# First experts in pairs of turns, with the weighted parts added by GpSimd

## The reference, cut to what matters

```python
def _L0_ffn_ref(x, gate_w, gate_b, w1, b1, w2, b2, gamma, beta):
    B, S, H, F, E, K = (8, 1024, 64, 128, 16, 2)
    gate_logits = x @ gate_w + gate_b
    topk_vals, topk_idx = jax.lax.top_k(gate_logits, K)
    topk_w = jax.nn.softmax(topk_vals, axis=-1)
    h = jax.nn.relu(jnp.einsum('bsh,ehf->bsef', x, w1) + b1)
    expert_out = jnp.einsum('bsef,efh->bseh', h, w2) + b2
    sel = jnp.take_along_axis(expert_out, topk_idx[:, :, :, None], axis=2)
    moe = jnp.sum(topk_w[..., None] * sel, axis=2)
    y = x + moe
    return layernorm(y) * gamma + beta
```

## Time and profile before

| what | value |
|---|---|
| runs shown, us | 741.77, 748.18, 747.81; median 747.81 |
| span of the profiled execution, us | 745.7 |
| TensorE busy, us (share) | 652.7 (88%) |
| VectorE busy | 570.2 (76%) |
| ScalarE busy | 502.8 (67%) |
| GpSimd busy | 334.1 (45%) |
| first experts: weightings L1132, 64 | 48.0 us busy, 750 ns each |
| first experts: VectorE's adds L1091, 56 | 44.1 us busy, 788 ns each on average |
| transfers mid<-spread_w, 128 | 128 KB each, 2.8 us from issue to landing |

### The profile page before, as it was taken

How to read it: one execution, slowest core, us unless ns; L and a number is a source line. 1 busy time by engine, 2 the same in 40 slices (tenths; PEclk the granted TensorE clock), 3 DMA queues, 4 the chain that set the end, 5 groups by cost and what they waited for, 6 DMA issues and landing times.

```text
span 745.7 us, 16401 instructions
## 1 busy us (share of the span) xinstructions
PE 652.7 (88%) x4984; PEld 364.3 (49%) x4984; DVE 570.2 (76%) x1633; ACT 502.8 (67%) x1264; POOL 334.1 (45%) x417
## 2 busy tenths in 40 slices
PE   5528998999999988999999997699888988889896
PEld 5514654666666654323333324365555655565332
DVE  6676787777777774798999988669888888867653
ACT  3746877888888872576777767658777777744542
POOL 1006578788787875133333333725445644320000
PEclk9857999999999997999999999699999999987999
DMA  4030000000000001433333330000000000000001
GB/s 109 1 113 1 1 2 1 0 0 0 0 0 0 1 0 66 161 106 108 109 113 115 107 109 14 3 1 2 1 0 0 0 0 0 1 1 1 16 20 23
DMA packets 22038, 24.37 MB, mean 33 GB/s; under 512 B 12390, under 2 KB 12902, under 8 KB 21734
## 3 DMA queue, kind: packets, MB, share of 16 engines
q1 hardware_dynamic: 19751, 23.31, 10.3%
q10 hardware_dynamic: 2239, 0.49, 0.3%
HBM read 22.48 MB, written 1.31 MB: 32 GB/s over the span
## 4 chain that ended last, share of the span: by engine, by line
PE 59%; DVE 19%; issue 8%; ACT 4%; POOL 2%; DMA 1%; DVEq 0%; SPq 0%; ACTq 0%; POOLq 0%
PE ps L723 8%; PE ps L759 7%; PE ps L1551 5%; PE ps L641 4%; PE ps L1573 4%; PE ps L717 4%; DVE big L1091 4%; PE ps L652 3%; DVE big L2062 3%; DVE big L1132 2%; PE ps L1557 2%; PE ps L1802 2%; PE ps L709 2%; PE ps L1824 2%; PE ps L705 2%
## 5 line engine op out<-in xcount | busy, mean ns | idle before, releaser
L1338 POOL TENSOR_TENSOR big<-big 128x1024 f32<-128x1024 f32 x64 | 119.9, 1895 | 45.3 <-DVE big L1152 45.3
L939 ACT ACTIVATE big<-ps,big 128x255 f32<-128x255 f32 x256 | 117.3, 485 | 11.4 <-DVE big L1146 8.9
L901 ACT ACTIVATE big<-ps,b1s 128x512 f32<-128x512 f32 x128 | 80.3, 679 | 40.1 <-PE ps L641 38.9
L1146 DVE TENSOR_REDUCE big<-ps 128x4 f32<-128x1020 f32 x64 | 75.2, 1213 | 27.3 <-PE ps L717 27.3
L1920 ACT ACTIVATE big<-ps 128x1024 f32<-128x1024 f32 x64 | 65.9, 1030 | 32.9 <-PE ps L1563 30.5
L2062 DVE TENSOR_REDUCE big<-ps 128x4 f32<-128x1020 f32 x64 | 78.1, 1220 | 6.8 <-DVE res L2119 2.5
L723 PE MATMUL ps<-cst,big 128*128 128x128 f32 x512 | 77.5, 285 | 6.3 <-POOL big L1338 2.4
L1158 DVE COPY mid<-ps 128x512 f32<-128x512 f32 x96 | 63.5, 686 | 18.7 <-PE ps L723 15.4
L641 PE MATMUL ps<-big,wall 64*128 64x512 f32 x256 | 75.7, 656 | 0.7 <-ACT big L872 0.7
L723 PEld LDWEIGHTS ps<-cst,big 128*128 128x128 f32 x512 | 54.9, 141 | 40.8 <-issue 20.8
L652 PE MATMUL ps<-big,w2s 128*64 128x512 f32 x256 | 70.8, 632 | 1.2 <-ACT big L901 1.2
(11 more groups left out here) (274 smaller groups left out, 1342.2 us busy)
## 6 DMA issues: line engine op xcount, KB each, us to landing
mid<-spread_w SPq DMA_DIRECT2D x128, 128.0 KB, 2.8
mid<-in_split_sel SPq DMA_DIRECT2D x1, 1536.0 KB, 7.5
wall<-in_w SPq DMA_DIRECT2D x1, 1280.0 KB, 6.2
out_tokens<-res SPq DMA_DIRECT2D x16, 56.0 KB, 1.6
cst<-in_consts SPq DMA_DIRECT2D x1, 520.5 KB, 5.1
pexp<-in_w_raw SPq DMA_DIRECT2D x1, 512.0 KB, 6.2
w2s<-in_w SPq DMA_DIRECT2D x1, 512.0 KB, 3.4
mid<-in_taps ACTq DMA_DIRECT2D x1, 320.0 KB, 3.9
```

What stands on the lines that cost most here:

```text
L901: last = nc.scalar.activation(hid[e % 2][j], H1(e, j), ACT.Relu, bias=b1s[0][:, 2 * e + j:2 * e + j + 1])
L939: last = nc.scalar.activation(e_sb[r % 4][:, jj, tq, 0:NW], S[:, 2 * (r % 2) + jj, tq, 0:NW], ACT.Exp, scale=-1.0, bias=minus[r % 4][:, jj ...
L1146: nc.vector.tensor_reduce(minus[r % 4], S[:, 2 * a:2 * a + 2, :, 0:NW], AX.X, ALU.min).then_inc(s_mx, 1)
L1338: nc.gpsimd.tensor_tensor(e_sb[r % 4], e_sb[r % 4], bc(inverse[r % 4].unsqueeze(3), [P, 2, 2, 256]), ALU.mult).then_inc(s_A, 1)
```

## The change

The diff, cut to its core. First the buffers and TensorE:

```diff
-            TURN_SUM, COLUMNS, LOGITS, GAP, WEIGHTS = 1, 6, 0, 2, 6
+            PARTS, ADDS = 4, DUOS - 1
+            GAP = 3
             tile = lambda first, n=512: big[:, first:first + n]
-            hid = [[tile(1024 * e + 512 * j) for j in range(2)] for e in range(2)]
-            part, acc = ([tile(2048 + 1024 * m + 512 * n) for n in range(2)] for m in range(2))
+            hid = [[tile(first + 512 * j) for j in range(2)] for first in (0, 1024, 4352, 5376)]
+            part = [tile(first) for first in (2048, 2560, 7936, 8448)]
+            acc = [tile(3072 + 512 * n) for n in range(2)]
...
                 def sum_turn(c, q, last_chunk=False):
-                    pe.wait_ge(s_acc, c + 1)
+                    pe.wait_ge(s_added, ADDS * (c + 1))
...
                 def duos(c, q):
                     known = isinstance(c, int)
-                    for e in range(DUOS):
-                        s = DUOS * c + e
-                        if e < DUOS - 1:
-                            hidden(q, e + 1, s + 1)
-                        elif not known or c < CH - 1:
-                            pe.wait_ge(s_xc, c + 2)
-                            hidden(1 - q, 0, s + 1)
-                        if e == WEIGHTS and (not known or c < CH - 1):
+                    for g in range(DUOS // 2):
+                        s = DUOS * c + 2 * g
+                        if g == DUOS // 2 - 1 and (not known or c < CH - 1):
                             weights(c + 1)
-                        second(e, s)
-                        if e == COLUMNS and (not known or c < CH - 2):
-                            if known and c == 0:
-                                pe.wait_ge(s_O, B)
-                            columns_of(c + 2)
-                        if e == LOGITS and (not known or c < CH - 1):
+                            if not known or c < CH - 2:
+                                if known and c == 0:
+                                    pe.wait_ge(s_O, B)
+                                columns_of(c + 2)
+                        for e in (2 * g + 2, 2 * g + 3):
+                            if e < DUOS:
+                                hidden(q, e, DUOS * c + e)
+                            elif not known or c < CH - 1:
+                                pe.wait_ge(s_xc, c + 2)
+                                hidden(1 - q, e - DUOS, DUOS * c + e)
+                        if g == 0 and (not known or c < CH - 1):
                             logits(c + 1, 1 - q)
-                        if e == TURN_SUM and (not known or c >= 1):
+                        second(2 * g, s)
+                        second(2 * g + 1, s + 1)
+                        if g == 0 and (not known or c >= 1):
                             sum_turn(c - 1, 1 - q, known and c == CH - 1)
```

ScalarE's `duos`: with four `hid` buffers a ReLU waits for the second product four turns back; the gap's exponential goes behind turn 3, the own scaling to turns 6 and 7, the copies of weights and columns behind turn 7:

```diff
-                        if not known or s >= 2:
-                            act.wait_ge(s_w2, s - 1)
+                        if not known or s >= 4:
+                            act.wait_ge(s_w2, s - 3)
...
-                        if e == 5 and c >= 1:
-                            own_scale(c - 1, (0, 1))
-                        if e == WEIGHTS and (not known or c < CH - 1):
+                        if e in (6, 7) and c >= 1:
+                            own_scale(c - 1, ((0, 1), (2, 3))[e - 6])
...
+                        if e == 7 and c < CH - 1:
                             weights(c + 1, 1 - q)
-                        if e == 6 and c >= 1:
-                            own_scale(c - 1, (2, 3))
+                        if e == 7 and c < CH - 2:
+                            columns_out(c + 2, q)
```

VectorE's `duos`, which no longer adds:

```diff
-                        if e == 1 and c >= 1:
-                            dve.wait_ge(s_acc, c)
-                        nc.vector.scalar_tensor_tensor(out=acc[q] if e == 0 else part[e % 2], in0=Y(e), scalar=b2s[:, e:e + 1], in1=cb[e % RING],
+                        n = ADDS * c + e - 1
+                        if e >= 1 and n >= PARTS:
+                            dve.wait_ge(s_added, n - PARTS + 1)
+                        nc.vector.scalar_tensor_tensor(out=acc[q] if e == 0 else part[n % PARTS], in0=Y(e), scalar=b2s[:, e:e + 1], in1=cb[e % RING],
                                                        op0=ALU.add, op1=ALU.mult).then_inc(s_m, 1)
-                        if e >= 2:
-                            add_part(c, q, e - 1)
-                        elif e == 0 and c >= 1:
-                            add_part(c - 1, 1 - q, DUOS - 1)
```

GpSimd's `duos`:

```diff
+                def add_part(c, e):
+                    n = ADDS * c + e - 1
+                    pool.wait_ge(s_m, DUOS * c + e + 1)
+                    if e >= 2:
+                        pool.wait_ge(s_added, n)
+                    nc.gpsimd.tensor_tensor(acc[c % 2], acc[c % 2], part[n % PARTS], ALU.add).then_inc(s_added, 1)
+
                 def duos(c):
                     if c < CH - 2:
                         fetch_chunk(c + 2)
+                    add_part(c, 1)
+                    add_part(c, 2)
                     if c >= 1:
                         own_root(c - 1)
+                    add_part(c, 3)
...
                     for h in ((0, 1), (2,), (3,), (4,), (5,), (6,), (7,), ())[c]:
                         pos_scores(h)
+                    add_part(c, 4)
+                    add_part(c, 5)
                     if c >= 2:
                         next_root(c - 2)
+                    add_part(c, 6)
+                    add_part(c, 7)
```

More of the change, by code:

```diff
@@ L582, in attention0_and_experts0 @@
             zb = small[:, 5:5 + H]
-            s_h, s_hid, s_w2, s_m, s_acc = (sem("e0_" + n) for n in ("hidden", "activated", "second_done", "weighted", "summed"))
+            s_h, s_hid, s_w2, s_m, s_added = (sem("e0_" + n) for n in ("hidden", "activated", "second_done", "weighted", "part_added"))
             s_cd, s_cb = sem("e0_weights_in_dram"), [sem(f"e0_spread{n}") for n in range(RING)]
@@ L651, in second @@
                     for j in range(2):
-                        last = nc.tensor.matmul(Y(e)[D * j:D * j + D], w2s[0][:, 2 * e + j], hid[e % 2][j], start=True, stop=True)
+                        last = nc.tensor.matmul(Y(e)[D * j:D * j + D], w2s[0][:, 2 * e + j], hid[e % 4][j], start=True, stop=True)
                     last.then_inc(s_w2, 1)
                 def sum_turn(c, q, last_chunk=False):
-                    pe.wait_ge(s_acc, c + 1)
+                    pe.wait_ge(s_added, ADDS * (c + 1))
                     if not last_chunk:
@@ L840, in _ @@
                 weights(0)
+                hidden(0, 1, 1)
                 duos(0, 0)
@@ L897, in duos @@
                         act.wait_ge(s_h, s + 1)
-                        if not known or s >= 2:
-                            act.wait_ge(s_w2, s - 1)
+                        if not known or s >= 4:
+                            act.wait_ge(s_w2, s - 3)
                         for j in range(2):
-                            last = nc.scalar.activation(hid[e % 2][j], H1(e, j), ACT.Relu, bias=b1s[0][:, 2 * e + j:2 * e + j + 1])
+                            last = nc.scalar.activation(hid[e % 4][j], H1(e, j), ACT.Relu, bias=b1s[0][:, 2 * e + j:2 * e + j + 1])
                         last.then_inc(s_hid, 1)
[L903 to L907, removed]
                         if e in (1, 2) and c >= 3:
@@ L911, in duos @@
                             gap(c + 1)
-                        if e == 5 and c >= 1:
-                            own_scale(c - 1, (0, 1))
-                        if e == WEIGHTS and (not known or c < CH - 1):
+                        if e in (6, 7) and c >= 1:
+                            own_scale(c - 1, ((0, 1), (2, 3))[e - 6])
+                        if e in (3, 7) and c >= 1:
+                            for h in (((0,), (1,)) if c == 1 else ((c,), ()))[e // 4]:
+                                pos_exps(h)
+                        if e == 7 and c < CH - 1:
                             weights(c + 1, 1 - q)
-                        if e == 6 and c >= 1:
-                            own_scale(c - 1, (2, 3))
+                        if e == 7 and c < CH - 2:
+                            columns_out(c + 2, q)
                 def columns_first():
@@ L1086, in finish @@
                     return [total, stats, own.variance, gain, add]
[L1088 to L1095, removed]
                 def pos_max(h):
@@ L1269, in _ @@
                     duos(c, c % 2)
-                add_part(CH - 1, 1, DUOS - 1)
                 later.finish, later.next_norm = finish, next_norm
```

## The result

Four runs of each kernel on one chip gave 761.8 us after the change (757.0 to 764.2) and 744.8 before (741.4 to 748.2): a ratio of 1.0222, 95% interval 1.018 to 1.0264. The change makes the kernel slower: the whole interval lies above 1. The profiled execution of after has a span of 762.3 us against 745.7, 16.6 more.

A forecast was written before the change was run, and what follows sets the result against it. TensorE and VectorE were both taken as nearly full. 745.7 + 12.5 (six loops) + 2 (chunk 0) = 760.2 us profiled; the median lies 2.1 above the span, so 762. Forecast's own range 756 to 767, overall 747 to 776.

The forecast's parts named there:

- The two holds: VectorE's L455 and shares' step wait for GpSimd's adds 2 and 3 on SBUF: +0.81 and +1.12 us per loop.
- The stall moved from the sum's turn to the weights' turn: TensorE, counted from S, the sum's turn's start: ready at 9.29, waits for weights; loop 20.5 us without holds, 22.4 with.
- Putting products side by side I cost at nothing: First experts on TensorE: pairing first and second products saves nothing; a pair of turns keeps four products, floor 19.58 per chunk.
- a first product behind a first product well under 1.06: Sign on TensorE that, if seen in the profile, would show the forecast wrong altogether.
- Little idle before the sum's turn: Profile sign on TensorE: little idle there, the next S coming 10.48 us after the weights' turn.
- the second rival: More than the loop: clock falls, GpSimd's 10.6 us chain and VectorE steps up to 0.3 each add time; 767 to 778, chance 0.22.
- The clock: Part of the more-than-the-loop case: TensorE's idle drops it to half speed, six falls of 1.7 us, +10, giving 772.
- Six loops: First to seventh sum's turn: 133.9 us against 121.4, so +12.5.
- Chunk 0: GpSimd's position scores hold the spread's eight small steps again and again: 0 to 3 us, taken as +2.
- Chunk 7: Last chunk, no weights to turn; GpSimd's adds now set its end: 0, give or take 2 us.
- the 762: Forecast median for the whole changed kernel in us; its case, 756 to 767, had chance 0.50.

The follow-up runs named there:

- run 9: Changed kernel with the position score ahead and adds 2 and 3 on VectorE behind the weights' spread: 736.5 us, 0.986 of the kernel before.
- run 3: Changed kernel with GpSimd's adds 2 and 3 moved behind the weights' spread, position score ahead of them: 743.7 us, 0.997 of the kernel before.
- second profile: Changed kernel run again unaltered, as a control in the second series: 757.4 us, 1.014 of the kernel before.
- run 1: Changed kernel with the 56 adds back on VectorE, new order of products kept: 752.6 us, 1.012 of the kernel before.
- run 2: Kernel before, its order of products kept, with the adds on GpSimd and four part buffers: 747.0 us, 1.001 of the kernel before.
- run 7: Changed kernel with adds 2 and 3 late and GpSimd's root for the next layer behind add 7: 762.1 us, 1.024 of the kernel before.

## Why the prediction was right, and where it wasn't

**The two holds: right, and shown.** The prediction gave L455 0.81 and the shares' step 1.12 more than 0.16; measured are 0.87 and 0.89 to 0.90, 1.76 together against 1.93. The second was over-sized by 0.22. GpSimd's root was done sooner than reckoned: add 3 started 0.09 behind weighting 3 instead of 0.29, and so ended sooner beside the step that it held; and the sum let that step run its 0.16 behind the add, while it ended 0.02 behind it; that the step was ready 0.13 earlier worked the other way. L455 averages 0.90 in the six loops (near 1.0 forecast): 1.03 on the path, 0.74 for the next layer's norm, which the position score's product holds up. GpSimd is busy 399.6 in all (406). The sentence on the Trainium skill's page "SBUF — State Buffer", section "Who interferes with whom", is borne out by these rows (1.03 and 1.06 for steps of 0.16, each ending with GpSimd's add). So, for the weighting, is its exemption of a VectorE instruction that has at most one SBUF input and isn't in a two-port mode: 749 ns on average in the six loops of before and of after, and 0.75 beside GpSimd's score (at 394.88).

**"The stall moved from the sum's turn to the weights' turn": right.** Weights were forecast at S + 11.79 and were there at 11.17; TensorE was forecast ready at 9.29 and was at 9.02; idle 2.6 forecast, 2.2 measured, six times, by the releaser that was named.

**"Putting products side by side I cost at nothing": wrong.** This is the step that failed. A pair of first products takes 0.20 less than two single ones, a pair of second ones 0.15 less: 4 x 0.35 = 1.4 per chunk. TensorE's own work in a loop is 18.05 (run 9: 19.22 of one loop less the 0.91 and 0.26 that it idles), not 19.58. The prediction had named a first product behind a first product well under 1.06 as a sign that it would be wrong altogether. The sign came (0.96 each), and the forecast stood all the same, because the part of this gain that lies ahead of the weights' turn was swallowed by the wait there, and the part behind it by the wait for GpSimd. Where the wait was taken away it came out: run 3 was forecast with a loop of 20.5 to 20.9 and had 19.95.

**"Little idle before the sum's turn": wrong.** From the weights' turn the prediction had 10.48 to the next S; 10.63 were measured in the loop shown, but of other parts: TensorE needs 9.40, and then waits 1.23 for GpSimd (0.8 on average in the six loops). That is GpSimd's chain of 10.6 in the second rival (from the spread's end at 393.67 to 404.31 it took 10.64), which the forecast treated as one that would add to the loop; it took the place of the gain of the pairs instead. Of the up to 0.3 that the rival gave each VectorE step in between, 0.32 came in all: adds 4 and 5 took 2.82 instead of 2.68, and the root's first step 1.20 instead of 1.02.

**The clock: a rival that came in part.** Six falls of 1.7 were its price; with six equal waits of 2.2 came two that cost 1.05 each (three in the second profile), and none where products filled the waits. The 1.7 is about right where no other wait takes up the loss (1.65 in run 1).

**The sum.** Six loops were to cost 12.5 and cost 9.5 (10.1 in the second profile). Chunk 0 was to cost 2. What it cost in all can't be read: the first sum's turn came at 317.70 and 321.65 in two profiles of one kernel, and at 318.55 before, where 10.2 us of that chunk (from 288.9) ran at half clock. But its mechanism is there. The spread in chunk 0, first before, then after, and TensorE's turn of the weights that waits for it:

```profile
305.57 1.68 DVE L1049 TENSOR_SCALAR big<-cst,big 128x16 f32<-128x16 f32 x8
```

```profile
302.33 3.79 DVE L1052 TENSOR_SCALAR big<-cst,big 128x16 f32<-128x16 f32 x8
...
306.44 0.60 PE L629 MATMUL ps<-cst,big 128*16 128x128 f32 x4 [3.82 <-DVE big L1054]
```

The eight small steps took 2.1 us longer beside GpSimd's scores, and TensorE idled 3.82 us (3.83 in the second profile, none before). Chunk 7, 0 give or take 2, was 1.75 and 0.1. That the median of the first series, 761.8, met the 762 is partly luck: the tail of some executions gave what the loops did not. The loops alone, 9.5 to 10.1 us on the 747.8 that the prediction started from, speak for 757 to 758, which the second series has (757.4).

## What to carry to other kernels

Before an elementwise step goes from VectorE to GpSimd, look at what VectorE does in the next microsecond: a tiny step with two SBUF operands on the critical chain pays for the rest of the other engine's add (0.9 of 1.27 us here), and the engines' busy times do not show whether anything waits for it. A hold is almost free as long as the result is wanted no sooner than it comes (run 2) and costs its full length once an order wants it sooner (after); so price both halves of a change together, not one by one. Where holds can't be avoided, put the long adds into the part of the loop in which nobody waits for the other engine's small steps, and look up who waits for each step that is moved (run 7).

## What the runs showed of the hardware that was not expected

Four products of 64x128x512 take 1.06 us between products of another kind, and eight of them in a row 1.92: the second four add 0.86. For the second products it is 1.01 and 1.87, so 0.86 again. Run 1, with the adds on VectorE, has TensorE busy 18.16 in a loop in the new order, and run 2, with the adds on GpSimd, 19.76 in the old one, so it is the order and not the adds. Why a change of kind costs this was not tested.

Not only steps with two tensors from SBUF are held. In chunk 0 of after the eight steps of the spread (L1052, 128x16, one tensor from SBUF and two columns of scalars) took 3.79 instead of 1.68 beside GpSimd's score, and a cast of 128x8 (L1037) that takes 0.17 elsewhere took 0.75 (299.40 to 300.15), beside an add that ran until 300.12. The kernel before had such meetings too: its add L1091, 0.68 by itself, took 1.13 at 351.39 beside the score's product.

TensorE's clock did not fall after each equal wait: of six idle times of 2.2 us, two were followed by a stretch of 3.4 us at half clock (1.2 GHz) in one profile (from 372.1 and 416.4) and three in the other (from 355.6, 420.5 and 444.4), partly in other loops. The first of them, columns as in the earlier trace rows:

```profile
372.10:375.50 3.40, 3.40 (x10) 1.19 (x8) 2.05 (x10) 1.98 (x4) 3.20 (x4) 0.50 0.05 12
```

What picks them stays open.
